# Graph attention over 200,000 edges: the one-hot matrix of the sums moves from matmul and ScalarE to compares on GpSimd, and queries shrink from 16 to 15 columns a head

## The chip, the cores and the metric

The kernel runs on one core of a Trainium2 chip. The metric is the device time of one execution in microseconds (us). A core has five engines that run beside each other and meet at semaphores: TensorE (PE in the profile, with PEld for its weight loads), VectorE (DVE), ScalarE (ACT), GpSimd (POOL) and SyncE (SP), which here only starts transfers. Sixteen DMA engines move data between HBM and SBUF.

## What is computed

A graph has 6250 nodes with 128 features and 200,000 edges with 128 features; `src` and `dst` name the ends of each edge, and the edges are sorted by `dst`. There are 8 heads of 16 columns.

```python
q = layer_norm(einsum('nf,hfd->hnd', x_node, Wq), gq, bq)      # k, v likewise; ke, ve from x_edge
rel_k = layer_norm(concatenate([ke, k[:, src]], -1) @ relk_W + relk_b, relk_g, relk_beta)
qk = sum(q[:, dst] * rel_k, -1) / 4.0
m = segment_max(qk.T, dst); se = segment_sum(exp(qk.T - m[dst]), dst)
lse = log(se) + m
rel_v = layer_norm(concatenate([ve, v[:, src]], -1) @ relv_W + relv_b, relv_g, relv_beta)
logw = qk - lse.T[:, dst]
agg = segment_sum(logw[..., None] * rel_v, dst)
z = layer_norm(relu(agg @ z_W + z_b), z_g, z_beta)
out = layernorm(x + z)
```

The inner layer norms remove the mean, so a head of 16 columns is held as 15 (`C = D - 1`, `HC = 8 * 15 = 120`). The 16th column of a query held the constant of the score, the part that comes from `relk_beta` and is the same for all edges of a node.

## The kernel before

Three phases follow each other: `start` (node projections, ranks, tables), `edges` (the loop over all edges) and `tail` (log-sum-exp, the folding of the sums, the output).

**The edge loop.** Edges are taken in 391 groups of 512 (`GROUPS`, four tiles of 128 edges). Each engine runs the same routine, `body(c)`, for one step after another, written out by hand in a fixed order; in step c it works on group c, c-1, ... as the pipeline asks. `PEEL` = 25 steps are written out, then a loop of 12 steps a turn, then the rest. Waits are semaphore counts; buffers are rings (`OR` = 6 one-hot matrices, `HR` = 6 results `hh`, `WR` = 4 weights `zw`).

For a group: PE transposes the edge features (L1159) and projects them twice (L1137). DVE scales the second projection to `p` (L1415), adds the gathered rows of the source nodes (L1395, group c-5), multiplies the key half by the expanded query (L1405, c-6), reduces sums of squares and products together (L1427, c-6), builds `hh`, which is what is summed over edges (L1432, c-9), and reduces the squares of the first projection (L1442, c-2). ACT squares, copies out of PSUM, and does the logarithms and exponentials.

**Queries by rank.** Within a tile the destination nodes are consecutive ranks. A DMA loads 128 rows of `q_by_rank` per tile (three bf16 parts each, `3 * F` = 384 columns), and 12 matmuls a group (L1195) expand them to edges with the one-hot matrix `oht` (ranks down, edges across), which one matmul (L1150) codes and ACT's Relu (L1225) makes.

**The sums.** The other orientation, `oh` (edges down, ranks across), serves as the weights of the matmuls that add `hh` up by rank (L1130, c-10). Before, four matmuls (L1188) code it in PSUM from three feature rows, and ACT's Relu (L1260) writes it to SBUF.

**GpSimd's step.** In `body(c)` GpSimd issues two indirect gathers (L1317, group c-3), multiplies the score into the weight, `w2` (L1330, c-9), forms the score without its constant, `qk0` (L1337, c-8), and issues the other two gathers of group c-3. DVE then adds the constant, which lies in column 15 of the product (L1389, c-9), and L1330 waits for that; DVE's L1432 waits for L1330:

```python
x = c - 9    # DVE, first in its step
v.tensor_tensor(out=hh[:, x % HR, :, :, 2 * C], in0=qk0[:], in1=z[:, x % ZR, :, 2 * H:3 * H, C], op=ALU.add)
...
dve.wait_ge(s_w2, n + 1)    # ahead of L1432
```

**In `start`**, nodes go in 25 pairs of 128-row blocks: ACT writes the first two bf16 parts of the query (L832, L839), and GpSimd scatters them to `q_by_rank` (L479). **In `tail`**, DVE forms `lse` in 13 turns (L1755).

Of the kernel before, what the change touches and what calls it, by code (L numbers as in the profile page):

```python
# [5 lines left out]
P = 128  # L6
# [42 lines left out]
def edge_attention(nc, a, out):  # L49
    f32, bf16, i32, u32 = mybir.dt.float32, mybir.dt.bfloat16, mybir.dt.int32, mybir.dt.uint32  # L50
    ctx = ExitStack()
    with ctx:
# [7 lines left out]
        q_rank = dram("q_by_rank", [QROWS, 3 * F], bf16)  # L60
# [35 lines left out]
        rank_i = sb_mid("first_rank", [1, ROWS], i32)  # L96
        nfeat = sb_mid("rank_code", [P, P], bf16)
# [5 lines left out]
                          first_pos=first_pos, sum_idx=sum_idx, degree=degree, carry_idx=carry_idx, w_edge=w_edge, cols=cols, rank_i=rank_i, nfeat=nfeat, feat=feat))  # L103
        def sb_late(name, shape, dt=f32):
# [7 lines left out]
                          w_edge=w_edge, cols=cols, rank_i=rank_i, nfeat=nfeat, feat=feat, eps_c=eps_c))  # L112
# [3 lines left out]
                         ones_row=ones_row, rows16=rows16, end_pos=end_pos, first_pos=first_pos, sum_idx=sum_idx, degree=degree), out)  # L116
# [21 lines left out]
def start(nc, a, t):  # L138
# [88 lines left out]
    room_b = sb("room_b", [P, BLOCKS * 3 * F // 2])  # L227
# [3 lines left out]
    qp = room_b[:].bitcast(bf16).rearrange("p (b f) -> p b f", f=3 * F)  # L231
# [23 lines left out]
    zero_q = sb("zero_q", [P, 3 * F], bf16)  # L255
# [9 lines left out]
    q1 = sb("n_q1", [P, 2, 2, F])  # L265
# [27 lines left out]
    s_u, s_tb, s_qs, s_q = sem("nodes_scaled"), sem("nodes_table"), sem("nodes_q_scaled"), sem("nodes_q")  # L293
    s_1, s_r1, s_2, s_3 = sem("nodes_part1"), sem("nodes_rest1"), sem("nodes_part2"), sem("nodes_part3")
# [23 lines left out]
    with nc.allow_non_contiguous_dma(reason="small weight and index layouts"), nc.Block(no_gpsimd_drain=True) as block:  # L318
# [82 lines left out]
        def _(pool):  # L401
# [69 lines left out]
            pool.reg_add(last_row, rows_less_2, 1)  # L471
            pool.wait_ge(s_idx, 1)
# [14 lines left out]
        def _(dve):  # L487
# [204 lines left out]
            for c in range(NP + 6):  # L692
                n = c - 4
                if pair(n):
                    b, nb, rows = pair(n)
                    dve.wait_ge(s_q, n + 1)
                    dve.wait_ge(s_1, n + 1)
                    if n >= 2:
                        dve.wait_ge(s_2, n - 1)
                        dve.wait_ge(s_3, n - 1)  # L700
                    v.tensor_tensor(out=q1[0:rows, n % 2, 0:nb, :], in0=q[0:rows, n % 3, 0:nb, :], in1=qp[0:rows, b:b + nb, 0:F], op=ALU.subtract).then_inc(s_r1, 1)
                n = c - 5
                if pair(n):
# [3 lines left out]
                    v.tensor_tensor(out=qp[0:rows, b:b + nb, 2 * F:3 * F], in0=q1[0:rows, n % 2, 0:nb, :], in1=qp[0:rows, b:b + nb, F:2 * F], op=ALU.subtract).then_inc(s_3, 1)  # L707
# [10 lines left out]
                if pair(n):  # L718
# [8 lines left out]
                    if n >= 3:  # L727
                        dve.wait_ge(s_1, n - 2)
                        dve.wait_ge(s_r1, n - 2)
# [26 lines left out]
        def _(act):  # L756
# [44 lines left out]
            for c in range(NP + 5):  # L801
# [20 lines left out]
                if pair(n):  # L822
# [4 lines left out]
                    sc_.activation(xt[:, n % 2, 0:nb, 0:rows], x_ps[:, 0:nb * F].rearrange("p (c n) -> p c n", c=nb)[:, :, 0:rows], ACT.Copy).then_inc(s_xc, 1)  # L827
                n = c - 4
                if pair(n):
                    b, nb, rows = pair(n)  # L830
                    act.wait_ge(s_r1, n + 1)
                    sc_.activation(qp[0:rows, b:b + nb, F:2 * F], q1[0:rows, n % 2, 0:nb, :], ACT.Copy).then_inc(s_2, 1)  # L832
                n = c - 3
                if pair(n):
# [4 lines left out]
                    sc_.activation(qp[0:rows, b:b + nb, 0:F], q[0:rows, n % 3, 0:nb, :], ACT.Copy).then_inc(s_1, 1)  # L839
# [5 lines left out]
        def _(pe):  # L845
# [68 lines left out]
            for c in range(NP + 1):  # L914
# [13 lines left out]
                if pair(n):  # L928
# [6 lines left out]
                    last.then_inc(s_xt, 1)  # L935
                if c == LB_AT:
                    pe.wait_ge(s_lb, 1)
# [10 lines left out]
def edges(nc, a, t):  # L948
# [16 lines left out]
    p = sb("e_p", [P, PR, TILES, H, 2, D])  # L965
    z = sb("e_z", [P, ZR, TILES, 3 * H, D])
# [4 lines left out]
    qk0 = sb("e_qk0", [P, TILES, H])  # L971
# [73 lines left out]
    with nc.Block(no_gpsimd_drain=True) as block:  # L1045
        @block.sync
        def _(sp):
# [8 lines left out]
            def body(c, i, loop):  # L1056
                if is_group(c, loop):
# [11 lines left out]
                    if c % BATCH == 0:  # L1069
                        b, kb = batch(c, i), (c // BATCH) % FB  # L1070
                        if loop or c >= BATCH * FB:
# [4 lines left out]
                            sp.wait_ge(s_ohp, used)  # L1076
# [38 lines left out]
        def _(pe):  # L1115
# [25 lines left out]
            def body(c, i, loop):  # L1141
                x = c - 4
                if is_group(x, loop):
                    n, kb = UNROLL * i + x, (x // BATCH) % FB
                    pe.wait_ge(s_ft[kb], 32 * (i + (x // BATCH) // FB + 1))
                    if loop or x >= 2:
                        pe.wait_ge(s_oh, n - 1)
                    elif x == 1:
                        pe.wait_ge(s_oht, 1)
# [31 lines left out]
                if is_group(x, loop):  # L1181
                    n, k, kb = UNROLL * i + x, x % QR, (x // BATCH) % FB
                    pe.wait_ge(s_oht, n + 2 if loop or x < GROUPS - 1 else n + 1)
                    if not loop and x == GROUPS - 1:
                        pe.wait_ge(s_oh, n)
# [949 lines left out]
```

## Time and profile before

| | us |
|---|---|
| median of 3 runs (lowest, highest) | 3037.59 (3036.09, 3039.39) |
| the profiled execution, its own time | 3036.29 |
| its span, first to last instruction | 3034.5 |
| DVE busy in the span | 2902.0 (96%) |
| PE busy in the span | 2843.7 (94%) |
| POOL busy in the span | 2407.3 (79%) |
| ACT busy in the span | 2306.7 (76%) |

Times of instructions come from the profiled execution. A row of the timeline gives start, duration, engine, line of the kernel, operation and operands, and in brackets the idle time ahead of it with what ended it. The recorded duration of an instruction reaches past the start of the next on the same engine (a DVE instruction of 960 elements is recorded at 1.15 to 1.34 us, and the next starts 1.07 us after it), so what an instruction costs its engine is the distance from start to start.

### The profile page before, as it was taken

What the parts mean: (1) busy time and instruction counts of PE and PEld (TensorE: products, weight loads), DVE (VectorE), ACT (ScalarE), POOL (GpSimd) and SP (SyncE); (2) the same over time, 40 slices, a digit from 0 to 9 for tenths busy, and PEclk for the clock granted to TensorE, in tenths of its full rate; (3) what the DMA queues carried; (4) which work ended last, traced back from release to release, by engine and by line L of the source; (5) the groups of instructions that cost most, each with busy time, mean ns of one, the idle gap of its engine ahead of it and who ended that gap; (6) DMA issues with size and microseconds to landing.
All of it is one profiled execution on the core that took longest, in us unless ns stands there. A gap on an engine that the chain in (4) does not pass through costs nothing. (4 is left out here: it accounts for less than half of the span.)

```text
span 3034.5 us, 76156 instructions
## 1 busy us (share of the span) xinstructions
PE 2843.7 (94%) x18870; PEld 2519.9 (83%) x18870; DVE 2902.0 (96%) x3459; ACT 2306.7 (76%) x5276; POOL 2407.3 (79%) x2622
## 2 busy tenths in 40 slices
PE   4669999999999999999999999999999999997945
PEld 3349999999999999999999999999999999995633
DVE  6879999999999999999999999999999999997957
ACT  2448888888888888888888888888888888885536
POOL 5768888888888888888888888888888888883773
PEclk9889999999999999999999999999999999998966
DMA  3568888888888888888888888888888888886642
GB/s 88 160 184 245 258 259 252 260 253 258 255 256 257 256 258 256 254 258 255 258 254 257 257 254 257 254 257 254 256 257 254 257 254 257 255 260 213 152 121 75
DMA packets 660921, 715.95 MB, mean 236 GB/s; under 512 B 97993, under 2 KB 554430, under 8 KB 660469
## 3 DMA queue, kind: packets, MB, share of 16 engines
q1 hardware_dynamic: 568201, 499.33, 52.3%
q0 software_dynamic: 84896, 211.42, 27.0%
q10 hardware_dynamic: 7756, 4.43, 0.6%
q8 instruction: 26, 0.43, 0.1%
q14 instruction: 42, 0.34, 0.0%
HBM read 482.62 MB, written 231.46 MB: 235 GB/s over the span
## 5 line engine op out<-in xcount | busy, mean ns | idle before, releaser
L1317 POOL DMA_INDIRECT e_rows<-node_table,e_gcol x1564 | 1933.0, 1236 | 422.6 <-issue 306.6
L1137 PE MATMUL banks<-w_edge,e_eat 128*128 128x240 f32 x6256 | 1396.5, 367 | 0.8 <-ACT e_ysq L1246 0.7
L1137 PEld LDWEIGHTS banks<-w_edge,e_eat 128*128 128x128 f32 x6256 | 1190.7, 191 | 87.6 <-issue 1.2
L1130 PE MATMUL banks<-e_h,e_oh 128*128 128x248 f32 x3128 | 805.5, 380 | 3.8 <-DVE e_h L1432 3.6
L1427 DVE TENSOR_REDUCE e_zs<-e_z 128x96 f32<-128x1440 f32 x391 | 671.6, 1718 | 0.2
L1130 PEld LDWEIGHTS banks<-e_h,e_oh 128*128 128x128 f32 x3128 | 534.6, 191 | 36.6 <-DVE e_h L1432 6.4
L1216 ACT ACTIVATE e_agg<-banks 128x496 f32<-128x496 f32 x782 | 453.8, 580 | 90.0 <-PE banks L1130 89.8
L1415 DVE TENSOR_TENSOR e_p<-banks,e_yr 128x960 f32<-128x960 f32 x391 | 479.4, 1226 | 5.0 <-PE banks L1137 4.3
L1395 DVE TENSOR_TENSOR e_p<-e_p,e_rows 128x960 f32<-128x960 f32 x391 | 479.6, 1227 | 0.0
L1432 DVE TENSOR_TENSOR e_h<-e_p,e_zw 128x960 f32<-128x960 f32 x391 | 478.5, 1224 | 1.2 <-POOL e_zw L1330 1.2
L1442 DVE TENSOR_REDUCE e_yvar<-e_ysq 128x64 f32<-128x960 f32 x391 | 477.2, 1221 | 0.0
L1225 ACT ACTIVATE e_oht<-banks 128x512 bf16<-128x512 f32 x391 | 233.4, 597 | 313.6 <-PE banks L1150 312.8
L1246 ACT ACTIVATE e_ysq<-banks 128x960 f32<-128x960 f32 x391 | 379.2, 970 | 51.5 <-PE banks L1137 6.4
L1239 ACT ACTIVATE e_z<-e_p 128x960 f32<-128x960 f32 x391 | 389.9, 997 | 6.1 <-DVE e_p L1395 5.0
L1195 PE MATMUL banks<-e_q,e_oht 128*128 128x128 bf16 x4692 | 326.5, 220 | 2.0 <-DVE e_z L1405 2.0
L1405 DVE TENSOR_TENSOR e_z<-e_p,banks 128x512 f32<-128x512 f32 x391 | 295.6, 756 | 0.1
L1195 PEld LDWEIGHTS banks<-e_q,e_oht 128*128 128x128 bf16 x4692 | 278.9, 98 | 2.5 <-issue 2.3
L1159 PEld LDWEIGHTS banks<-ident,e_ea 128*128 128x128 f32 x1564 | 195.5, 141 | 93.5 <-DMA e_ea<-in_edge_attr 24.2
L1159 PE MATMUL banks<-ident,e_ea 128*128 128x128 f32 x1564 | 235.8, 274 | 22.3 <-DMA e_ea<-in_edge_attr 22.3
L1231 ACT ACTIVATE e_eat<-banks 128x512 f32<-128x512 f32 x391 | 231.6, 592 | 17.5 <-PE banks L1159 17.4
L1260 ACT ACTIVATE e_oh<-banks 128x512 f32<-128x512 f32 x391 | 229.5, 587 | 0.0
L1188 PE MATMUL banks<-rank_code,e_feat 128*128 128x128 bf16 x1564 | 151.5, 220 | 0.0
(413 smaller groups left out, 2691.1 us busy)
## 6 DMA issues: line engine op xcount, KB each, us to landing
tile_sums<-e_agg SPq DMA_DIRECT2D x391, 496.0 KB
e_q<-q_by_rank SPq DMA_DIRECT2D x1564, 96.0 KB
e_ea<-in_edge_attr SPq DMA_DIRECT2D x390, 256.0 KB
e_rows<-node_table,e_gcol POOLq DMA_INDIRECT x1564
edge_lse<-t_lse_sb SPq DMA_DIRECT2D x14, 448.0 KB, 3.8
edge_qk<-e_qkt SPq DMA_DIRECT2D x130, 48.0 KB
node_table<-n_tb SPq DMA_DIRECT2D x24, 240.0 KB, 2.7
n_x<-in_x SPq DMA_DIRECT2D x24, 128.0 KB, 2.2
```

Of the source, the lines that this page charges most:

```text
L1130: last = nc.tensor.matmul(sums_bank(x, loop, half)[:, (j % 2) * AW:(j % 2 + 1) * AW], oh[:, x % OR, j, :], hh[:, x % HR, j, :, :].rearrang ...
L1137: last = nc.tensor.matmul(out_ps[:, j // 2, (j % 2) * 2 * HC:(j % 2 + 1) * 2 * HC], eat[:, x % 4, j * P:(j + 1) * P], t["w_edge"][:, at:at ...
L1159: last = nc.tensor.transpose(eat_ps[:, j * P:(j + 1) * P], ea[:, k, j, :], ident[:])
L1195: last = nc.tensor.matmul(qx_ps[:, j * F:(j + 1) * F], oht[:, x % 2, j * P:(j + 1) * P], qw[:, k, j, part * F:(part + 1) * F], start=(part ...
L1216: nc.scalar.activation(agg[:, k, 2 * half:2 * half + 2, :].rearrange("p j c -> p (j c)"), sums_bank(x, loop, half)[:, 0:2 * AW], ACT.Copy) ...
L1239: nc.scalar.activation(z[:, x % ZR, :, 0:2 * H, 0:C], p[:, k, :, :, :, 0:C].rearrange("p t h k c -> p t (h k) c"), ACT.Square).then_inc(s_ ...
L1317: g.indirect_dma_start(out=rows[:, k, j, :], out_offset=None, in_=table, in_offset=bass.IndirectOffsetOnAxis(ap=gcol[:, kb, at:at + 1].bit ...
L1395: v.tensor_tensor(out=p[:, k, :, :, :, 0:C].rearrange("p t h k c -> p (t h k) c"), in0=p[:, k, :, :, :, 0:C].rearrange("p t h k c -> p (t ...
L1415: v.tensor_tensor(out=p[:, k, :, :, :, 0:C].rearrange("p (b t) h k c -> p b (t h k) c", b=2), in0=u_ps.rearrange("p b (h c) -> p b h c", c=C),
L1427: v.tensor_reduce(out=zs[:, x % WR, :, :], in_=z[:, x % ZR, :, :, 0:C], axis=AX.X, op=ALU.add).then_inc(s_z, 1)
L1432: v.tensor_tensor(out=hh[:, x % HR, :, :, 0:2 * C].rearrange("p t h (s c) -> p (t h) s c", s=2), in0=p[:, k, :, :, 1, 0:C].rearrange("p t ...
L1442: v.tensor_reduce(out=yvar[:, x % 2, :, :], in_=ysq[:, x % 2, :, :].rearrange("p t (h c) -> p t h c", c=C), axis=AX.X, op=ALU.add).then_in ...
```

## The change

1. **One-hot by compare.** `start` keeps each edge's rank within its tile as bytes, edges down the partitions (`ranks`): 13 PE transposes in 4 sets, an ACT copy for each set, and two small fills by GpSimd. The edge loop loads 12 columns of them per batch of three groups (a third small DMA beside those for `feat` and `gcol`), ACT turns them to fp32 once a batch (`rcol`), and GpSimd makes `oh` with four `tensor_scalar` compares a group of a row 0..127 against each edge's rank. The four coding matmuls and ACT's Relu for it go.
2. **15 columns.** `q_by_rank` holds `3 * HC` = 360 columns, the expanded query 480 columns a group and not 512, and DVE's product L1405 works on 480.
3. **The constant by node.** DVE's add L1389 goes; GpSimd's product writes the score straight into `hh`. `start` keeps the constant of each node (`q_beta`, one small ACT copy per pair), and `tail` adds and subtracts it in `lse` (two more small DVE instructions a turn).

```diff
@@ start
+                if 0 <= k4 < RANK_SETS:
+                    act.wait_ge(s_rkt, k4 + 1)
+                    sc_.activation(t["ranks"][:].rearrange("e (p k) -> e k p", k=KT)[:, k0:k1, :],
+                                   bank[7][:, 0:(k1 - k0) * P].rearrange("e (k p) -> e k p", p=P), ACT.Copy).then_inc(s_rkc, 1)
...
+                    sc_.activation(t["q_beta"][0:rows, b:b + nb, :], q4[:, :, :, C], ACT.Copy).then_inc(s_qb, 1)
...
+                    for k in range(4 * k4, min(4 * k4 + 4, KT)):
+                        last = nc.tensor.transpose(bank[7][:, (k % 4) * P:(k % 4 + 1) * P], rank[:, k, :], ident[:])
@@ edges, SyncE
+                        sp.dma_start(rcol_i[:, kb, :], t["ranks"][:, bass.ds(BATCH * TILES * b, BATCH * TILES)]).then_inc(s_ft[kb], 16)
@@ edges, TensorE
-                    for j in range(TILES):
-                        at = (x % BATCH) * GE + j * P
-                        last = nc.tensor.matmul(misc[:, j * P:(j + 1) * P], feat[:, kb, at:at + P], t["nfeat"][:], start=True, stop=True)
-                    last.then_inc(s_ohp, 1)
...
-                            last = nc.tensor.matmul(qx_ps[:, j * F:(j + 1) * F], oht[:, x % 2, j * P:(j + 1) * P],
-                                                    qw[:, k, j, part * F:(part + 1) * F], start=(part == 0), stop=(part == 2))
+                            last = nc.tensor.matmul(qx_ps[:, j * HC:(j + 1) * HC], oht[:, x % 2, j * P:(j + 1) * P],
+                                                    qw[:, k, j, part * HC:(part + 1) * HC], start=(part == 0), stop=(part == 2))
@@ edges, ScalarE
-                    nc.scalar.activation(oh[:, x % OR, :, :].rearrange("p j n -> p (j n)"), misc, ACT.Relu).then_inc(s_oh, 1)
+                if is_group(x, loop) and x % BATCH == 0:
...
+                    nc.scalar.activation(rcol[:, kb, :], rcol_i[:, kb, :], ACT.Copy).then_inc(s_rf, 1)
@@ edges, GpSimd (after L1330)
+                x = c - 7
+                    pool.wait_ge(s_rf, batch(x, i) + 1)
+                    if loop or x >= OR:
+                        pool.wait_ge(s_agg, 2 * (n - OR) + 2)
                 x = c - 8
                     pool.wait_ge(s_zr, n + 1)
-                    g.tensor_tensor(out=qk0[:], in0=zs[:, x % WR, :, 2 * H:3 * H], in1=zr[:, x % WR, :, 0:H], op=ALU.mult).then_inc(s_qk0, 1)
+                    g.tensor_tensor(out=hh[:, x % HR, :, :, 2 * C], in0=zs[:, x % WR, :, 2 * H:3 * H], in1=zr[:, x % WR, :, 0:H], op=ALU.mult).then_inc(s_qk, 1)
+                x = c - 7
+                    for j in range(TILES):
+                        last = g.tensor_scalar(out=oh[:, x % OR, j, :], in0=iota_r[:], scalar1=rcol[:, kb, at + j:at + j + 1], scalar2=None, op0=ALU.is_equal)
+                    last.then_inc(s_oh, 1)
                 gathers(c - 3, i, loop, 2)
@@ edges, VectorE
-                    v.tensor_tensor(out=hh[:, x % HR, :, :, 2 * C], in0=qk0[:], in1=z[:, x % ZR, :, 2 * H:3 * H, C], op=ALU.add).then_inc(s_qk, 1)
...
-                                    in1=qx_ps.rearrange("p (t h d) -> p t h d", t=TILES, d=D), op=ALU.mult).then_inc(s_pq, 1)
+                                    in1=qx_ps[:, 0:TILES * HC].rearrange("p (t h c) -> p t h c", t=TILES, c=C), op=ALU.mult).then_inc(s_pq, 1)
@@ tail, VectorE
-                    v.tensor_tensor(out=lse[rr, 0:nb, :], in0=l0[rr, 0:nb, :], in1=lln[rr, 0:nb, :], op=ALU.add).then_inc(s["lse"], 1)
+                    v.tensor_tensor(out=lsr[rr, 0:nb, :], in0=l0[rr, 0:nb, :], in1=lln[rr, 0:nb, :], op=ALU.add).then_inc(s["lsr"], 1)
+                    dve.wait_ge(s["lsr"], n + 1)
+                    v.tensor_tensor(out=lsf[rr, 0:nb, :], in0=lsr[rr, 0:nb, :], in1=qb, op=ALU.add).then_inc(s["lsf"], 1)
+                    dve.wait_ge(s["lsf"], n + 1)
+                    v.tensor_tensor(out=lse[rr, 0:nb, :], in0=lsf[rr, 0:nb, :], in1=qb, op=ALU.subtract).then_inc(s["lse"], 1)
```

## Rows read from the trace of the kernel before

**Rows 1.** Busy time by stage, the steady part of the edge loop.

```profile
232.00:2746.00 2514.00, 2512.45 (x17387) 2287.16 (x17386) 2513.31 (x2689) 2072.20 (x4732) 2092.56 (x2305) 1.00 0.86 256
```

The columns are the window, its length, the busy us (and instructions) of PE, PEld, DVE, ACT and POOL, the granted TensorE clock, the busy share of the DMA engines, and GB/s.

**Rows 2.** Timeline of DVE over one step of the loop.

```profile
1498.87 1.34 DVE L1395 TENSOR_TENSOR e_p<-e_p,e_rows 128x960 f32<-128x960 f32 x1
1499.94 0.87 DVE L1405 TENSOR_TENSOR e_z<-e_p,banks 128x512 f32<-128x512 f32 x1
1500.53 1.34 DVE L1415 TENSOR_TENSOR e_p<-banks,e_yr 128x960 f32<-128x960 f32 x1
1501.60 1.83 DVE L1427 TENSOR_REDUCE e_zs<-e_z 128x96 f32<-128x1440 f32 x1
1503.16 1.34 DVE L1432 TENSOR_TENSOR e_h<-e_p,e_zw 128x960 f32<-128x960 f32 x1
1504.23 1.33 DVE L1442 TENSOR_REDUCE e_yvar<-e_ysq 128x64 f32<-128x960 f32 x1
1505.30 0.39 DVE L1389 TENSOR_TENSOR e_h<-e_qk,e_z 128x32 f32<-128x32 f32 x1
1505.42 1.34 DVE L1395 TENSOR_TENSOR e_p<-e_p,e_rows 128x960 f32<-128x960 f32 x1
```

**Rows 3.** Timeline of POOL over the same step.

```profile
1501.12 0.30 POOL L1330 TENSOR_TENSOR e_zw<-e_h,e_zw 128x32 f32<-128x32 f32 x1
1501.36 0.26 POOL L1337 TENSOR_TENSOR e_qk<-e_zs,e_zr 128x32 f32<-128x32 f32 x1
1501.78 1.04 POOL L1317 DMA_INDIRECT e_rows<-node_table,e_gcol  x1 [0.16 <-issue]
1503.12 1.02 POOL L1317 DMA_INDIRECT e_rows<-node_table,e_gcol  x1 [0.30 <-issue]
1504.45 1.01 POOL L1317 DMA_INDIRECT e_rows<-node_table,e_gcol  x1 [0.30 <-issue]
1505.77 1.87 POOL L1317 DMA_INDIRECT e_rows<-node_table,e_gcol  x1 [0.30 <-DVE e_h L1389]
1507.66 0.29 POOL L1330 TENSOR_TENSOR e_zw<-e_h,e_zw 128x32 f32<-128x32 f32 x1
```

**Rows 4.** Timeline of POOL and DVE, the filling of the loop.

```profile
219.03 1.01 POOL L1317 DMA_INDIRECT e_rows<-node_table,e_gcol  x1 [0.30 <-issue]
219.15 1.15 DVE L1395 TENSOR_TENSOR e_p<-e_p,e_rows 128x960 f32<-128x960 f32 x1
...
229.92 2.08 POOL L1317 DMA_INDIRECT e_rows<-node_table,e_gcol  x1 [0.30 <-issue]
...
229.96 1.15 DVE L1395 TENSOR_TENSOR e_p<-e_p,e_rows 128x960 f32<-128x960 f32 x1
```

**Rows 5.** Timeline of POOL and DVE, the draining of the loop.

```profile
2765.00 0.28 POOL L1330 TENSOR_TENSOR e_zw<-e_h,e_zw 128x32 f32<-128x32 f32 x1 [1.22 <-DVE e_h L1389]
2765.31 1.16 DVE L1432 TENSOR_TENSOR e_h<-e_p,e_zw 128x960 f32<-128x960 f32 x1 [0.40 <-POOL e_zw L1330]
2765.89 0.69 POOL L1337 TENSOR_TENSOR e_qk<-e_zs,e_zr 128x32 f32<-128x32 f32 x1 [0.61 <-ACT e_zr L1290]
```

**Rows 6.** Timeline of POOL in the first phase.

```profile
8.95 0.29 POOL L419 TENSOR_SCALAR_AFFINE_SELECT ident<-ident 128x128 f32<-128x128 f32 x1
9.20 0.19 POOL L421 TENSOR_SCALAR_AFFINE_SELECT sent<-sent 128x2 f32<-128x2 f32 x1
...
10.03 0.20 POOL L428 MEMSET tri<- 128x128 f32 x1
10.17 0.20 POOL L429 MEMSET ones<- 128x128 f32 x1
```

**Rows 7.** Groups of instructions by line: node stage, then the tail's line by itself.

```profile
L832 ACT ACTIVATE room_b<-n_q 128x256 bf16<-128x256 f32 x21 | 8.7, 417 | 1.0 <-DVE n_q L701 1.0
...
L1755 DVE TENSOR_TENSOR t_x<-t_x x13: 166/182/183, 2920.0 to 3007.8; 128x32 f32<-128x32 f32 x12, 106x8 f32<-106x8 f32 x1
```

In the second line the three numbers are the shortest, median and longest duration in ns.

More of the change, by code:

```diff
@@ L706, in _ @@
                     dve.wait_ge(s_2, n + 1)
-                    v.tensor_tensor(out=qp[0:rows, b:b + nb, 2 * F:3 * F], in0=q1[0:rows, n % 2, 0:nb, :], in1=qp[0:rows, b:b + nb, F:2 * F], op=ALU.subtract).then_inc(s_3, 1)
+                    v.tensor_tensor(out=qp[0:rows, b:b + nb, 2 * HC:3 * HC], in0=q1[0:rows, n % 2, 0:nb, :], in1=qp[0:rows, b:b + nb, HC:2 * HC], op=ALU.subtract).then_inc(s_3, 1)
                 n = c - 3
@@ L728, in _ @@
                         dve.wait_ge(s_1, n - 2)
+                        dve.wait_ge(s_qb, n - 2)
                         dve.wait_ge(s_r1, n - 2)
@@ L831, in _ @@
                     act.wait_ge(s_r1, n + 1)
-                    sc_.activation(qp[0:rows, b:b + nb, F:2 * F], q1[0:rows, n % 2, 0:nb, :], ACT.Copy).then_inc(s_2, 1)
+                    sc_.activation(qp[0:rows, b:b + nb, HC:2 * HC], q1[0:rows, n % 2, 0:nb, :], ACT.Copy).then_inc(s_2, 1)
                 n = c - 3
@@ L935, in _ @@
                     last.then_inc(s_xt, 1)
+                k4 = c - RANK_TURN
+                if 0 <= k4 < RANK_SETS:
+                    if k4 == 0:
+                        pe.wait_ge(s_wev, WEIGHTS)
+                        pe.wait_ge(s_rank, 1)
+                    else:
+                        pe.wait_ge(s_rkc, k4)
+                    for k in range(4 * k4, min(4 * k4 + 4, KT)):
+                        last = nc.tensor.transpose(bank[7][:, (k % 4) * P:(k % 4 + 1) * P], rank[:, k, :], ident[:])
+                    last.then_inc(s_rkt, 1)
                 if c == LB_AT:
+                    pe.wait_ge(s_rkc, RANK_SETS)
                     pe.wait_ge(s_lb, 1)
@@ L1182, in body @@
                     n, k, kb = UNROLL * i + x, x % QR, (x // BATCH) % FB
-                    pe.wait_ge(s_oht, n + 2 if loop or x < GROUPS - 1 else n + 1)
-                    if not loop and x == GROUPS - 1:
-                        pe.wait_ge(s_oh, n)
-                    for j in range(TILES):
-                        at = (x % BATCH) * GE + j * P
-                        last = nc.tensor.matmul(misc[:, j * P:(j + 1) * P], feat[:, kb, at:at + P], t["nfeat"][:], start=True, stop=True)
-                    last.then_inc(s_ohp, 1)
+                    pe.wait_ge(s_oht, n + 1)
                     pe.wait_ge(s_q[k], 64 * use(x, i, QR))
@@ L1238, in body @@
                         act.wait_ge(s_z, n - ZR + 1)
-                    nc.scalar.activation(z[:, x % ZR, :, 0:2 * H, 0:C], p[:, k, :, :, :, 0:C].rearrange("p t h k c -> p t (h k) c"), ACT.Square).then_inc(s_psq, 1)
+                    nc.scalar.activation(z[:, x % ZR, :, 0:2 * H, :], p[:, k, :, :, :, :].rearrange("p t h k c -> p t (h k) c"), ACT.Square).then_inc(s_psq, 1)
                 x = c - 1
@@ L1330, in body @@
                     g.tensor_tensor(out=zw[:, x % WR, :, :, 1], in0=hh[:, x % HR, :, :, 2 * C], in1=zw[:, x % WR, :, :, 0], op=ALU.mult).then_inc(s_w2, 1)
+                x = c - 7
+                if is_group(x, loop):
+                    n = UNROLL * i + x
+                    if not loop and x == 0:
+                        pool.wait_ge(s_iota, 1)
+                    pool.wait_ge(s_rf, batch(x, i) + 1)
+                    if loop or x >= OR:
+                        pool.wait_ge(s_agg, 2 * (n - OR) + 2)
                 x = c - 8
@@ L1352, in link @@
                 dve.wait_ge(s_ch, done[0])
-            dve.wait_ge(s_k, 5)
+            dve.wait_ge(s_k, 6)
+            v.tensor_copy(out=iota_r[:], in_=r_i).then_inc(s_iota, 1)
+            dve.wait_ge(s_iota, 1)
             link(v.tensor_tensor(out=ends[:, 1:2], in0=t["ends_f"][:, 1:2], in1=t["ends_f"][:, 0:1], op=ALU.not_equal))
@@ L1509, in tail @@
     la, ld = [small() for _ in range(2)], [small() for _ in range(2)]
-    lab, lex, lln, l0, lse = (small() for _ in range(5))
+    lab, lex, lln, l0, lsr, lsf, lse = (small() for _ in range(7))
     var, lnv = (small() for _ in range(2))
```

112 lines of the change are left out of this document (62 added, 50 removed).

## The prediction

> **What bounds the kernel now.** I read the busy time by stage first: the steady part of the edge loop is 2514 us of a span of 3034.5 us, and in it DVE is busy 2513.31 us [rows 1]. Its 2689 DVE instructions are 7 a step, so there are 384 steps of 2514 / 384 = 6.547 us. PE shows as much (2512.45 us), but its ends are modelled; ACT has 2072.20 us and POOL 2092.56 us, with clock 1.00 throughout. Then the timeline of DVE over one step [rows 2]: seven instructions without a gap, from start to start 1.07 (L1395), 0.59 (L1405), 1.07 (L1415), 1.56 (L1427), 1.07 (L1432), 1.07 (L1442) and 0.12 (L1389), together 6.55. DVE bounds the loop.
>
> The page makes POOL look 79% busy, with a fifth of its time to give. The timeline of POOL over the same step [rows 3] says otherwise. It has no wait for a partner's data: L1330 takes 0.24, L1337 with the gap behind it 0.42, then gathers at distances of 1.34, 1.33 and 1.32 (each 1.0 busy and 0.30 "issue", which the busy figure leaves out), and a fourth of 1.89. The only elastic part is that fourth, recorded at 1.87 where the others take 1.02. It starts at 1505.77, inside DVE's L1395, which runs from 1505.42 for 1.07. The timeline of the filling shows the same when POOL comes at other phases [rows 4]: a gather that starts 0.12 ahead of L1395 takes 1.01, one that starts 0.04 ahead takes 2.08. So a POOL instruction whose read of SBUF falls into a DVE instruction with two SBUF inputs stands still until that has finished. The draining shows it for an ordinary POOL instruction against L1432, the other DVE instruction of that kind [rows 5]: L1337 takes 0.69 and not 0.26, ending at 2766.58, 0.20 after L1432's 1.07 us are over. Without such a stop POOL's step is 0.24 + 0.42 + 1.34 + 1.33 + 1.32 + 1.05 = 5.70 us (1.05 is the free gather of 1.02 with the 0.02 or 0.03 that follows it): true slack 0.85 us a step, less what the stops take.
>
> The Trainium skill (SBUF — State Buffer, "Who interferes with whom") has this rule: a VectorE instruction with two SBUF inputs contends with a GpSimd instruction that reads SBUF, and whichever is second waits for the whole of the first. The rows agree for POOL as the second (0.69 for 0.26). The rule speaks against putting more reading instructions on POOL; without it the sum would be the third case below.
>
> **The change part by part.**
>
> *DVE.* L1389 goes, 0.12 a step. L1405 falls from 512 to 480 elements; between it and L1395, 448 elements make 1.07 − 0.59 = 0.48, so 32 make 0.03. DVE's step becomes 6.55 − 0.15 = 6.40: 384 × 0.147 = 56 us less, if DVE stays the bound.
>
> *PE and ACT.* PE loses four coding matmuls and 8 of 128 columns in twelve others, ACT an eviction of 512 columns a group against one tiny conversion per three groups. Neither sets the step; I give both nothing, and the saving only leaves them more room. PE's busy share falls if the step grows; at clock 1.00 it has room even then.
>
> *SP and DMA.* One more small load per three groups, rows of 720 bytes and not 768. The loads run ahead by several groups: nothing.
>
> *POOL.* Four compares of 128x128 are added. The trace has none. Nearest is the affine select of 128x128, one input and no second: 0.25 from its start to the next instruction [rows 6]. Below lies a fill of the same size, which reads nothing, 0.14; above, something beyond 0.25 for fetching a scalar per partition, for which the trace has no row; I take up to 0.40, half more than the select, as the upper bound. With 0.25: the free step becomes 5.70 − 0.42 + 0.24 + 4 × 0.25 + 0.16 = 6.68 (the 0.16 is the gap ahead of a gather). That is over DVE's 6.40 before any stop. POOL becomes the bound unless a compare costs under (6.40 − 5.68) / 4 = 0.18 all told.
>
> *Where the stalls go.* With POOL late, what is late next is DVE's L1432, which waits for L1330. Behind it on DVE stand L1442 and the next L1395. Take L1330's start as zero. L1432 starts at 0.31 [rows 5] and holds the read until 1.38. POOL's score product, at 0.24, is already under way. The first compare would start at 0.48, inside L1432: it stands until 1.38. Then four compares of 0.25 end at 2.38, and the gather is ready at 2.38 + 0.16 = 2.54. Meanwhile DVE has gone on: L1432, L1442, then L1395 from 0.31 + 2 × 1.07 = 2.45. The gather comes 0.09 too late and stands behind L1395: it ends 2.04 after L1395's start, as in the filling (2.08 from 0.04 ahead), at 4.49. Then 0.30 of issue, 1.33, 1.32 and the free 1.05 bring the next L1330 to 8.49. So the step is 8.49 us and repeats itself: DVE has only 6.40 us of work and waits 2.1 us each time at L1432, then starts the very instruction that stops the compares. The compare's cost drops out of this sum within bounds: the gather escapes only if it starts 0.12 ahead of L1395, so 1.38 + 4C + 0.16 below 2.33, C below 0.20; and if C is over (2.45 − 1.38) / 3 = 0.36, the last compare also falls behind L1395. The 0.04 or so that the first compare may need after the stop, and L1330's own variations, are within 0.2 us a step; the range of this case is 8.3 to 9.1 (at C = 0.40: 3.52 + 0.40 + 0.16 + 1.34 + 1.33 + 1.32 + 1.05 = 9.12).
>
> On the price of a compare the Trainium skill (GPSIMD Engine Reference, "Elementwise — side-by-side cycle accounting") gives 1.8 cycles at 1.2 GHz for each element in a tight loop, so as an estimate 128 × 1.8 / 1.2 = 192 ns and dispatch on top; no run here shows a compare. By that alone the sum would be the same, since C would stay between the two bounds.
>
> *Start and tail.* `start` gains 25 small ACT copies and four larger ones. If all were on the path at L832's 0.417, that is 12 us; DVE's part gets 16 columns narrower. `tail` gains 26 DVE instructions of 0.182 at most [rows 7], 4.7 us, in a stage where DVE often waits. I take 4 + 3 = 7 us, between 0 and 15.
>
> *The sum.* Against the profiled execution's own 3036.3 us (1.3 below the median, which is of no account here): 3036.3 + 384 × (8.49 − 6.547) + 7 = 3036.3 + 746 + 7 = 3789, and I say 3790.
>
> **The rivals.**
>
> *One stop, not two.* If compares cost under 0.20, or DVE resumes a little later so that the gather slips in ahead of L1395, only L1432's stop remains: with C = 0.20, 1.38 + 0.80 + 0.16 + 1.34 + 1.33 + 1.32 + 1.05 = 7.38; from 7.1 (C = 0.14) to 8.1 if steps of both kinds mix. Times 3256 to 3640, at 7.38 3363. For it: the margin is only 0.09 us. Against it: a compare has more to fetch than the select.
>
> *POOL bounds, without stops.* If compares, unlike the 32-element product, are not held up or only held for an instant, the step is 6.68 and the time 3036.3 + 384 × 0.133 + 7 = 3094. Against it: both kinds of POOL instruction in the rows were stopped.
>
> *The other side: faster.* The place is POOL's step: if a compare costs like a fill, 0.14, and the stops fall where a gather is already past its read, as the gather at 1503.12 is against L1432 at 1503.16 in rows 2 and 3, POOL needs 5.68 + 0.56 = 6.24, and DVE's 6.40 decides: 3036.3 − 56 + 7 = 2987. It decides below C = 0.18. Against it: L1330 and the compares are then four to six short reads in a row, and DVE's two instructions cover 2.14 of every 6.40 us.
>
> *No change.* The gain on DVE and a POOL step that happens to be 6.5 cancel: a narrow band.
>
> *Dearer compares.* C over 0.40 gives more than 4025 us.
>
> **How the numbers follow.** Chances: two stops 0.50; one stop 0.22; POOL without stops 0.10; faster 0.12; no change 0.02; dearer 0.04. The likeliest gives 3790, its own range is 3036.3 + 7 + 384 × (8.3 to 9.1 − 6.547), 3716 to 4024. Of the whole, a range from 3090, which takes in POOL's bound without stops, to 4030 leaves out the faster case, no change and the dearest, 0.18. A measurement of this kernel can tell about 0.2% from no change; faster by more than that 0.12, within it 0.02, slower 0.86.
>
> **What would show it.** If right, the profile after has DVE idle some 2 us a step ahead of L1432, released by POOL's L1330; POOL without a free moment beside its issue gaps; the first compare of four recorded at about 1.2 us and the others at about 0.3; one gather of four at about 2.0; PE and ACT idle a quarter. The compares' distances give C itself. If compares run at 0.14 to 0.18 and DVE stays gapless at 6.40, the prediction is wrong at the price of a compare; if they cost 0.25 but never show 1 us, it is wrong at the stop; if DVE waits for gathered rows and not for L1330, the phase that I worked out, and so the 8.49, is wrong.

## The result and the profile after

The kernel after takes 4258.19 us (4254.99 to 4260.55, 4 runs) where the kernel before takes 3037.78: 1.4018 of it, 95% interval 1.4000 to 1.4035. The direction was forecast, the size was not: 3790 us, with 4030 as the upper end. A step of the edge loop went from 6.547 us to 9.70 us; 384 × (9.70 − 6.547) = 1211 us, and that is all but 10 of the difference.

Four lines of the page of the kernel after; the groups are line, engine, operation and operands, then busy us and mean ns, then the idle time ahead with its releaser.

```profile
PE 3196.8 (75%) x17319; PEld 2655.6 (62%) x17319; DVE 3018.5 (71%) x3094; ACT 2170.2 (51%) x5045; POOL 3635.4 (85%) x4189
...
L1346 POOL DMA_INDIRECT e_rows<-node_table,e_gcol x1564 | 1624.9, 1039 | 425.2 <-issue 391.3
...
L1380 POOL TENSOR_SCALAR e_oh<-e_iota,e_rcol 128x128 f32<-128x128 f32 x1564 | 1549.3, 1001 | 0.0
...
L1467 DVE TENSOR_TENSOR e_h<-e_p,e_zw 128x960 f32<-128x960 f32 x391 | 594.3, 1520 | 1103.9 <-POOL e_zw L1359 1103.9
```

VectorE has fallen from 96% to 71%, and nearly all its idle time is one wait, 1103.9 us ahead of L1467 (L1432 before), for GpSimd's L1359 (L1330 before): 2.8 us a step. The compares are recorded at 1.0 us each. The gathers, which took 1236 ns on the mean, now take 1039: they are no longer the ones that are held.

The timeline of POOL over one step of the kernel after, to set beside [rows 3]:

```profile
2010.39 0.29 POOL L1359 TENSOR_TENSOR e_zw<-e_h,e_zw 128x32 f32<-128x32 f32 x1
2010.63 0.26 POOL L1375 TENSOR_TENSOR e_h<-e_zs,e_zr 128x32 f32<-128x32 f32 x1
2010.87 3.97 POOL L1380 TENSOR_SCALAR e_oh<-e_iota,e_rcol 128x128 f32<-128x128 f32 x4
2015.00 1.11 POOL L1346 DMA_INDIRECT e_rows<-node_table,e_gcol  x1 [0.17 <-issue]
2016.42 1.02 POOL L1346 DMA_INDIRECT e_rows<-node_table,e_gcol  x1 [0.30 <-issue]
2017.74 1.01 POOL L1346 DMA_INDIRECT e_rows<-node_table,e_gcol  x1 [0.31 <-issue]
2019.06 1.01 POOL L1346 DMA_INDIRECT e_rows<-node_table,e_gcol  x1 [0.30 <-issue]
2020.08 0.30 POOL L1359 TENSOR_TENSOR e_zw<-e_h,e_zw 128x32 f32<-128x32 f32 x1
```

POOL has no free moment beside its issue gaps; four compares fill 3.97 of 9.70 us. Whether that is their own cost or stops shows in shorter windows of POOL's timeline, which cut the merged row into single ones:

```profile
2010.87 0.61 POOL L1380 TENSOR_SCALAR e_oh<-e_iota,e_rcol 128x128 f32<-128x128 f32 x1
...
2010.87 1.85 POOL L1380 TENSOR_SCALAR e_oh<-e_iota,e_rcol 128x128 f32<-128x128 f32 x2
...
2011.46 1.84 POOL L1380 TENSOR_SCALAR e_oh<-e_iota,e_rcol 128x128 f32<-128x128 f32 x2
...
2013.28 1.55 POOL L1380 TENSOR_SCALAR e_oh<-e_iota,e_rcol 128x128 f32<-128x128 f32 x1
```

The group of these compares over the whole trace, by source line (shortest, median and longest ns):

```profile
L1380 POOL TENSOR_SCALAR e_oh<-e_iota,e_rcol x1564: 590/619/2248, 218.4 to 3981.5; 128x128 f32<-128x128 f32 x196
```

DVE's timeline of the same stretch, to set beside [rows 2]:

```profile
2010.72 1.52 DVE L1467 TENSOR_TENSOR e_h<-e_p,e_zw 128x960 f32<-128x960 f32 x1 [2.86 <-POOL e_zw L1359]
2012.17 1.14 DVE L1477 TENSOR_REDUCE e_yvar<-e_ysq 128x64 f32<-128x960 f32 x1
2013.23 1.14 DVE L1431 TENSOR_TENSOR e_p<-e_p,e_rows 128x960 f32<-128x960 f32 x1
2014.30 0.64 DVE L1440 TENSOR_TENSOR e_z<-e_p,banks 128x480 f32<-128x480 f32 x1
```

A compare that isn't held takes 0.59 from start to start (2010.87 to 2011.46). The second, from 2011.46, is held until L1467 ends at 2012.17, where the next VectorE instruction starts, and ends at 2012.72, 0.55 after it; the fourth starts at 2013.28, in L1431 (from 2013.23), and ends at 2014.83, 0.53 after it. VectorE loses as well: L1467 starts at 0.33 after L1359, but its successor comes 1.45 later and not 1.07, so it loses 0.38. So the walk for the kernel after, from L1359's start: product 0.24, first compare 0.48, L1467 really runs 0.71 to 1.78, second compare from 1.07, done at 2.31, third at 2.90, fourth held by L1431 (2.84 to 3.91), done at 4.44; then 0.17 and gathers at 4.61, 6.03, 7.35 and 8.67, and the next L1359 at 9.70. Compares of 0.59 and two stops of 0.64 and 0.96. The walk is fitted to this trace; the runs with two compares and with the compares last test it.

### The profile page after: what moved, and what is told of

Its sections match the earlier page's. It is cut to its first block and busy times, and to the rows that moved or that the text cites. A ratio compares the mean times of both kernels' runs of the same rounds, so it can differ in the third digit from the quotient of the medians.

```text
span 4255.3 us, 73823 instructions
## 1 busy us (share of the span) xinstructions
PE 3196.8 (75%) x17319; PEld 2655.6 (62%) x17319; DVE 3018.5 (71%) x3094; ACT 2170.2 (51%) x5045; POOL 3635.4 (85%) x4189
## 5 line engine op out<-in xcount | busy, mean ns | idle before, releaser
L1346 POOL DMA_INDIRECT e_rows<-node_table,e_gcol x1564 | 1624.9, 1039 | 425.2 <-issue 391.3
L1173 PE MATMUL banks<-w_edge,e_eat 128*128 128x240 f32 x6256 | 1597.8, 405 | 1.2 <-ACT e_ysq L1274 1.0
L1166 PE MATMUL banks<-e_h,e_oh 128*128 128x248 f32 x3128 | 943.1, 429 | 863.8 <-DVE e_h L1467 861.7
L1380 POOL TENSOR_SCALAR e_oh<-e_iota,e_rcol 128x128 f32<-128x128 f32 x1564 | 1549.3, 1001 | 0.0
L1173 PEld LDWEIGHTS banks<-w_edge,e_eat 128*128 128x128 f32 x6256 | 1341.6, 215 | 145.6 <-issue 1.6
L1467 DVE TENSOR_TENSOR e_h<-e_p,e_zw 128x960 f32<-128x960 f32 x391 | 594.3, 1520 | 1103.9 <-POOL e_zw L1359 1103.9
L1166 PEld LDWEIGHTS banks<-e_h,e_oh 128*128 128x128 f32 x3128 | 582.2, 207 | 998.4 <-issue 886.8
L1450 DVE TENSOR_TENSOR e_p<-banks,e_yr 128x960 f32<-128x960 f32 x391 | 447.5, 1144 | 4.1 <-PE banks L1173 4.1
L1431 DVE TENSOR_TENSOR e_p<-e_p,e_rows 128x960 f32<-128x960 f32 x391 | 446.8, 1143 | 1.0 <-DMA e_rows<-node_table,e_gcol 1.0
L1223 PE MATMUL banks<-e_q,e_oht 128*128 128x120 bf16 x4692 | 349.3, 231 | 4.7 <-DVE e_z L1440 4.2
L1440 DVE TENSOR_TENSOR e_z<-e_p,banks 128x480 f32<-128x480 f32 x391 | 250.6, 641 | 0.0
L1184 PE MATMUL banks<-e_feat,rank_code 128*128 128x512 bf16 x391 | 148.3, 379 | 0.0
```

The costliest lines, as they stand in the source:

```text
L1166: last = nc.tensor.matmul(sums_bank(x, loop, half)[:, (j % 2) * AW:(j % 2 + 1) * AW], oh[:, x % OR, j, :], hh[:, x % HR, j, :, :].rearrang ...
L1173: last = nc.tensor.matmul(out_ps[:, j // 2, (j % 2) * 2 * HC:(j % 2 + 1) * 2 * HC], eat[:, x % 4, j * P:(j + 1) * P], t["w_edge"][:, at:at ...
L1223: last = nc.tensor.matmul(qx_ps[:, j * HC:(j + 1) * HC], oht[:, x % 2, j * P:(j + 1) * P], qw[:, k, j, part * HC:(part + 1) * HC], start=( ...
L1346: g.indirect_dma_start(out=rows[:, k, j, :], out_offset=None, in_=table, in_offset=bass.IndirectOffsetOnAxis(ap=gcol[:, kb, at:at + 1].bit ...
L1380: last = g.tensor_scalar(out=oh[:, x % OR, j, :], in0=iota_r[:], scalar1=rcol[:, kb, at + j:at + j + 1], scalar2=None, op0=ALU.is_equal)
L1431: v.tensor_tensor(out=p[:, k, :, :, :, :].rearrange("p t h k c -> p (t h k c)"), in0=p[:, k, :, :, :, :].rearrange("p t h k c -> p (t h k ...
```

## The experiments

The experiments ran on four chips. On the first and the third the kernel before itself took longer (3223 us, 3182 to 3269 in 17 runs; 3154 us, 3145 to 3172 in 7) than on the second and the fourth (3036 and 3035 us). Steps that no transfer holds up can be compared across chips, the times of the first and third chip can't. A changed kernel whose time has no interval beside it ran once.

**A cheaper instruction in place of the compare: an affine select.**

```diff
-                        last = g.tensor_scalar(out=oh[:, x % OR, j, :], in0=iota_r[:], scalar1=rcol[:, kb, at + j:at + j + 1], scalar2=None, op0=ALU.is_equal)
+                        last = g.affine_select(out=oh[:, x % OR, j, :], in_=iota_r[:], compare_op=ALU.not_equal, fill=1.0, base=0, pattern=[[-1, P]], channel_multiplier=1)
```

> The kernel after, with each of the four compares replaced by an affine select of the same 128x128 (one input, 0.25 us in the trace of before; its result does not depend on the edge's rank, so the sums are not the reference's). Theory A, the prediction's walk with two stops: step 8.49 us, time about 3790 us. Theory A2, the same port rule with what the trace after shows in addition (VectorE's L1467 must itself wait until a compare's read is over, and is 0.4 us late): L1467 ends at 1.78 after L1359's start, only one select is held, the gather is ready at 2.64 and L1431 starts at 2.85, so one stop: step 7.68, time about 3480. Rival B (no port: POOL's own sum alone decides): step 6.68, time about 3100.

It took 3914.74 us on the first chip. The timeline of POOL over a step:

```profile
2009.16 0.30 POOL L1359 TENSOR_TENSOR e_zw<-e_h,e_zw 128x32 f32<-128x32 f32 x1
2009.40 0.27 POOL L1375 TENSOR_TENSOR e_h<-e_zs,e_zr 128x32 f32<-128x32 f32 x1
2009.61 1.99 POOL L1380 TENSOR_SCALAR_AFFINE_SELECT e_oh<-e_iota 128x128 f32<-128x128 f32 x4
2011.76 2.00 POOL L1346 DMA_INDIRECT e_rows<-node_table,e_gcol  x1 [0.16 <-issue]
2014.06 1.03 POOL L1346 DMA_INDIRECT e_rows<-node_table,e_gcol  x1 [0.30 <-issue]
2015.39 1.02 POOL L1346 DMA_INDIRECT e_rows<-node_table,e_gcol  x1 [0.31 <-issue]
2016.72 1.01 POOL L1346 DMA_INDIRECT e_rows<-node_table,e_gcol  x1 [0.30 <-issue]
2017.75 0.30 POOL L1359 TENSOR_TENSOR e_zw<-e_h,e_zw 128x32 f32<-128x32 f32 x1
```

The step is 8.59 us, where the prediction's walk has 8.49 and the walk with L1467 0.4 late has 7.68. Both stops are where they were predicted: four selects of 0.25 take 1.99 because L1467 holds the first, and the gather comes just too late and takes 2.00. My amendment of the walk was wrong for this instruction (L1467 is only 0.09 late here), and POOL's own sum, 6.68, is refuted.

**An instruction that reads nothing: a fill.**

```diff
+                        last = g.memset(oh[:, x % OR, j, :], 1.0)
```

> The kernel after, with each of the four compares replaced by a fill of the same size, which reads nothing (the one-hot matrix is all ones, so the sums are not the reference's). GpSimd's own step is 5.68 + 4 x 0.14 = 6.24 us, under VectorE's 6.40. Rival B (GpSimd's own sum and VectorE's alone): VectorE is the bound, step 6.40, time about 2990 us. Theory A (gathers stop behind VectorE instructions with two SBUF inputs): a slack of 0.16 us can't take a stop, so GpSimd still bounds, step 6.8 to 7.3, time 3140 to 3330.

It took 3383.25 us on the first chip, with a step of 7.21.

```profile
2013.16 0.30 POOL L1359 TENSOR_TENSOR e_zw<-e_h,e_zw 128x32 f32<-128x32 f32 x1
2013.40 0.27 POOL L1375 TENSOR_TENSOR e_h<-e_zs,e_zr 128x32 f32<-128x32 f32 x1
2013.59 0.64 POOL L1380 MEMSET e_oh<- 128x128 f32 x4
2014.39 1.22 POOL L1346 DMA_INDIRECT e_rows<-node_table,e_gcol  x1 [0.16 <-issue]
2015.91 1.80 POOL L1346 DMA_INDIRECT e_rows<-node_table,e_gcol  x1 [0.30 <-issue]
```

The fills themselves are not held, though L1467 runs over them; the gathers behind them are, 0.2 and 0.8 us. GpSimd's own sum was 0.16 below VectorE's, and it still became the bound: free slack under one stop is no slack.

**What in a compare costs 0.59?** Five kernels after with one thing changed each: the compare against a constant, a subtraction in its place, each compare as two of 64 columns, a plain copy, and the row 0..127 in bf16.

```diff
-... in0=iota_r[:], scalar1=rcol[:, kb, at + j:at + j + 1], scalar2=None, op0=ALU.is_equal)
+... in0=iota_r[:], scalar1=5.0, scalar2=None, op0=ALU.is_equal)
+... in0=iota_r[:], scalar1=rcol[:, kb, at + j:at + j + 1], scalar2=None, op0=ALU.subtract)
+... for half in (0, 64): out=oh[:, x % OR, j, half:half + 64], in0=iota_r[:, half:half + 64], ...
+last = g.tensor_copy(out=oh[:, x % OR, j, :], in_=iota_r[:])
+iota_r = sb("e_iota", [P, P], bf16)
```

> The kernel after, with the compare against the constant 5.0 and not against each edge's rank (so the one-hot matrix is not the reference's). Theory P (the 0.59 us of a compare come from fetching a scalar per partition): the compare falls to about 0.25 and the time to that of the select's run. Theory O (they come from the operation and its 128 elements): 0.55 to 0.6 as before, step 9.7, time about 4250 us.

> The kernel after, with the four compares as subtractions of the rank per partition (same operands, other operation; the one-hot matrix holds differences, so the sums are not the reference's). Theory O1 (the compare operation is what costs 0.59 against the affine select's 0.25): a subtraction costs 0.25 to 0.35, step about 8.5 to 8.7. Theory O2 (any tensor_scalar of this size costs it, whatever the operation): 0.59 and a step of 9.7.

> The kernel after, with each compare made as two of 64 columns (eight a group, same result). Cost fixed per instruction: eight cost twice as much as four, GpSimd's step grows by 2.4 us to about 12. Cost by element: an instruction of 64 costs a little over 0.3 us and the step stays within 0.5 of 9.7.

> The kernel after with each compare replaced by a plain copy of the same 128x128 (same input, no scalar; the one-hot matrix holds the numbers 0 to 127, so the sums are not the reference's). Theory S (the 0.53 to 0.59 us belong to tensor_scalar, not to reading and writing 128 elements): 0.25 a copy as for the affine select, and its step of 8.6. Rival R (any copy-like instruction of this size costs it): 0.5 and more, step 9.4 to 9.7.

> The kernel after with the row 0..127 that the compares read kept in bf16 (exact, same result). Rival: if the width of the input is part of a compare's 3 ns per element, a compare falls below 0.59 and the step below 9.5. Theory: it is the instruction's own loop, so 0.59 and 9.7 stay.

The group's own row in each of the five, in that order (shortest, median and longest ns):

```profile
L1380 POOL TENSOR_SCALAR e_oh<-e_iota x1564: 527/530/1548, 284.1 to 4163.1; 128x128 f32<-128x128 f32 x196
```

```profile
L1380 POOL TENSOR_SCALAR e_oh<-e_iota,e_rcol x1564: 592/621/2236, 221.2 to 3986.9; 128x128 f32<-128x128 f32 x196
```

```profile
L1381 POOL TENSOR_SCALAR e_oh<-e_iota,e_rcol x3128: 430/432/2378, 220.8 to 4440.1; 128x64 f32<-128x64 f32 x196
```

```profile
L1380 POOL COPY e_oh<-e_iota x1564: 279/283/1268, 219.8 to 3543.9; 128x128 f32<-128x128 f32 x196
```

```profile
L1380 POOL TENSOR_SCALAR e_oh<-e_iota,e_rcol x1564: 590/619/2247, 219.7 to 3982.2; 128x128 f32<-128x128 bf16 x196
```

| in place of the compare | time, us | step, us | median ns |
|---|---|---|---|
| (kernel after) | 4258.19 | 9.70 | 619 |
| constant, not a scalar per partition (first chip) | 4460.18 | 10.0 | 530 |
| subtraction | 4260.84 | 9.70 | 621 |
| two halves of 64 columns | 4713.23 | 10.86 | 432 |
| row 0..127 in bf16 | 4259.40 | 9.70 | 619 |
| plain copy | 3815.29 | 8.58 | 283 |

The cost is the instruction's, not the comparison's and not that of moving 128 elements: the affine select and the copy do the same elements for 0.23 to 0.25. The scalar per partition is no part of it either. With the constant the compare is recorded at 530 ns, but single rows of POOL's timeline show idle time between the compares, and from the second to the third start it is the same 0.59:

```profile
2011.51 1.34 POOL L1380 TENSOR_SCALAR e_oh<-e_iota 128x128 f32<-128x128 f32 x1
...
2012.91 0.53 POOL L1380 TENSOR_SCALAR e_oh<-e_iota 128x128 f32<-128x128 f32 x1
...
2013.50 1.46 POOL L1380 TENSOR_SCALAR e_oh<-e_iota 128x128 f32<-128x128 f32 x1
...
2015.02 0.53 POOL L1380 TENSOR_SCALAR e_oh<-e_iota 128x128 f32<-128x128 f32 x1
```

These rows also say why its step is 10.0 and not 9.70. The first compare starts 0.34 after L1375 where it is 0.24, the gap ahead of the gather is 0.28 where it is 0.17, and the two stops, now on the first and third compare, are 0.81 and 0.93 in place of 0.64 and 0.96.

A half that isn't held costs 0.41 from start to start:

```profile
2014.07 0.43 POOL L1381 TENSOR_SCALAR e_oh<-e_iota,e_rcol 128x64 f32<-128x64 f32 x1
...
2014.48 1.29 POOL L1381 TENSOR_SCALAR e_oh<-e_iota,e_rcol 128x64 f32<-128x64 f32 x1
```

So 64 elements cost 0.18 us, or 2.8 ns each, and 0.23 is fixed. The half-size run fell between its two expectations, since two fifths of a compare are fixed.

The runs differ in who gives way at L1467. Where the first instruction behind L1375 isn't held (the compare, the subtraction, the bf16 row), L1467 loses 0.38. Where that instruction is held (the constant, the halves, the copy, the select), L1467 loses 0.05 to 0.09. No run shows what decides it: the constant's compare starts 0.1 later than the kernel's own, but the first half starts at the same 0.47 after L1359 as the whole compare does, and is held.

The copy is also the prediction's sum at nearly its own price: 0.23 to 0.24 apiece, step 8.58, time 3815.29 us, where 8.49 and 3790 were forecast.

**Two compares in place of four.**

```diff
-                    for j in range(TILES):
+                    for j in range(2):
```

> The kernel after with two of the four compares a group (the other two quarters of the one-hot ring are filled with ones once, so the sums are not the reference's). Theory A, the walk with a compare at 0.59 and the port held by L1467 from 0.71 to 1.78 after L1359's start: second compare done at 2.31, gather ready at 2.47, ahead of L1431 at 2.84, so not held; the next gather at 3.81 held for 0.1 only; next L1359 at 7.56, time about 3430. Rival (four compares of 0.97 apiece, no stops: each compare costs its distance in the trace after): 9.70 - 2 x 0.97 = 7.76 with no gather of over 1.15 us; rival without any stop, at 0.59: 6.84, time about 3150.

The other two quarters of the ring are filled with ones once, ahead of the loop. The step is 7.58 us (L1360 at 2004.68 and 2012.26), as the walk has it, 7.56, where compares of 0.97 apiece without stops would have made it 7.76. No gather takes over 1.11 us. The time, 3525.46 us, is that of the third chip and can't be set against the 3430 expected.

**The four compares behind the second pair of gathers.**

```diff
+                gathers(c - 3, i, loop, 2)
                 x = c - 7
                 if is_group(x, loop):
...
-                gathers(c - 3, i, loop, 2)
```

> The kernel after with the four compares behind the second pair of gathers (same result). Theory A: the two stops stay but fall on gathers: ready at 0.66 and held by L1467 until 1.42, ready at 2.69 and held by L1431 until 3.56, then four compares of 0.59 unheld, step 9.45, about 4160 us; two gathers a step of 1.7 to 1.9 us and four compares together of 2.4. Rival (the compares themselves cost 0.97): still 4.0 us for the four, step 9.7 or over.

```profile
2008.02 0.29 POOL L1359 TENSOR_TENSOR e_zw<-e_h,e_zw 128x32 f32<-128x32 f32 x1
2008.26 0.26 POOL L1375 TENSOR_TENSOR e_h<-e_zs,e_zr 128x32 f32<-128x32 f32 x1
2008.67 1.79 POOL L1346 DMA_INDIRECT e_rows<-node_table,e_gcol  x1 [0.15 <-issue]
2010.76 1.79 POOL L1346 DMA_INDIRECT e_rows<-node_table,e_gcol  x1 [0.30 <-issue]
2012.60 2.35 POOL L1381 TENSOR_SCALAR e_oh<-e_iota,e_rcol 128x128 f32<-128x128 f32 x4
```

The step is 9.55 (9.45 expected), the time on the third chip 4283.19 us. The same two stops have moved to the gathers, and the four compares, unheld, take 2.35 us, 0.59 each. So 0.59 is theirs and the rest of the 3.97 was stops.

**The change without its first part.** The one-hot matrix comes again from four matmuls and a Relu; 15 columns and the constant by node are kept.

```diff
+                    for j in range(TILES):
+                        at = (x % BATCH) * GE + j * P
+                        last = nc.tensor.matmul(misc[:, j * P:(j + 1) * P], feat[:, kb, at:at + P], t["nfeat"][:], start=True, stop=True)
...
+                    nc.scalar.activation(oh[:, x % OR, :, :].rearrange("p j n -> p (j n)"), misc, ACT.Relu).then_inc(s_oh, 1)
...
-                        last = g.tensor_scalar(out=oh[:, x % OR, j, :], ...
```

> The change without its first part: the one-hot matrix again by four matmuls and ScalarE's Relu, no ranks in the first phase; queries of 15 columns and the constant by node kept. Theory: VectorE stays the bound and loses 0.15 us a step, GpSimd does as much as before: 3037 - 56 + 4 (start, tail) = 2985 us. Rival: GpSimd's score product, now ahead of L1432's data, or a stop at another phase costs more than the slack: 3037 or over.

> The kernel before, unchanged, for a profile beside the others of this call. Expected: VectorE without a gap, 6.55 us a step; if the loop shows waits for transfers here, they are the chip's and hold for its neighbours too.

> As in the first run without the compares (one-hot by matmul and Relu; 15 columns and the constant by node kept), with the kernel before profiled on the same chip. Theory: VectorE's step falls from 6.55 to 6.40 and the time by 1.5 to 2%. Rival: what VectorE gives back is taken up by waits for TensorE, for the eviction of the sums or for transfers, and the ratio stays within 0.5% of 1.

On the first chip the ratio was 1.0029 (0.9985 to 1.0073), inconclusive. On the second it was 3020.95 us against 3036.08: 0.9952 (0.9938 to 0.9965). The kernel before gave 3035.89 us there, so no transfer was in its way. Faster, but by 15 us and not by the 52 expected. The next four runs ask why.

**One coding matmul in place of four**, in the kernel without compares and in the kernel before:

```diff
-                    for j in range(TILES):
+                    for j in range(1):
                         at = (x % BATCH) * GE + j * P
```

> The kernel without the compares (15 columns and the constant by node kept), with one of its four coding matmuls a group (three quarters of the one-hot matrix then come from what stood in PSUM, so the sums are not the reference's): TensorE's step is 3 x 0.055 = 0.17 us shorter. Theory T (TensorE bounds it at 6.49, right behind VectorE's 6.40): the step falls to about 6.40 and the time to 2985 to 2990. Rival (VectorE's waits come from elsewhere, transfers or ScalarE): no change from 3021.

> The kernel before with one of its four coding matmuls a group (three quarters of the one-hot matrix then come from what stood in PSUM). Theory: VectorE bounds the kernel before at 6.55, so nothing changes: 3036 within 0.2%. Rival: TensorE bounds it as well, and it gets faster.

> As the earlier run with one coding matmul and no compares, which fell on a chip where the store of the sums held things up. Theory T: TensorE bounds the kernel without compares at 6.49 a step, so with 0.17 us less of it the step is 6.40 and the time 30 us under that of the next run. Rival: no difference between the two.

> The kernel without the compares once more, beside the run with one coding matmul: 0.995 of the kernel before where transfers are not in the way, as before.

On the third chip the first of these took 3216.21 us, 1.0193 (1.0141 to 1.0245) of the kernel before: a miss, with ScalarE's eviction of the sums (L1228) waiting 120.9 us in 1000 for a releaser that the profile calls remote; in the kernel the only such wait there is for the store of earlier sums. So it says nothing of TensorE. The kernel before with one coding matmul gave 3140.67 there in one run, 4 us under the lowest of the seven unchanged ones, which spread over 27: no gain that can be told. The median distance of its L1330 rows from 300 to 2700 us, 6.55, is that of the unchanged kernel's, 6.54. On the fourth chip the pair is clean: 2973.26 us, 0.9795 (0.9779 to 0.9812), against 3021.26 us, 0.9954 (0.9937 to 0.9970). The stretch from 300 to 2700 us in the windows view (PE, PEld, DVE, ACT, POOL busy; clock; DMA share; GB/s), without compares and then with one coding matmul:

```profile
300.00:2700.00 2400.00, 2400.00 (x16693) 2182.57 (x16692) 2380.41 (x2212) 1988.19 (x4543) 1997.55 (x2212) 1.00 0.87 254
```

```profile
300.00:2700.00 2400.00, 2392.29 (x15848) 2147.54 (x15847) 2399.82 (x2256) 2025.50 (x4627) 1984.64 (x2252) 1.00 0.88 258
```

In the first TensorE has no gap and VectorE has 20 us of them; in the second it is the other way round. TensorE's step without the compares is 6.51 us (2400 us for 2212 / 6 = 368.7 steps), just under VectorE's old 6.547, and that is where the gain ends. Between the two runs lie 48 us, where 30 were expected.

## Why the prediction was right and wrong

*VectorE the bound before, POOL's true step 5.70.* Right as far as the runs test it: without the compares the loop follows VectorE and TensorE, and POOL's step does not show.

*VectorE's saving, 0.15 a step.* Right: with TensorE out of the way the step is 6.38 (2400 / (2256 / 6)), where 6.40 was forecast. "Neither sets the step; I give both nothing" was wrong for TensorE in the part that I costed at nothing: in the kernel without compares its step is 6.51, 0.04 under VectorE's old one. It made no difference to the kernel after, where POOL decides, but it decides what parts 2 and 3 bring alone.

*The price of a compare: the step that failed.* "Nearest is the affine select of 128x128 ... 0.25", with "up to 0.40" as the upper bound. It is 0.59. The select was the right neighbour by shape, not by instruction: what set the price was tensor_scalar's own 2.8 ns an element. What the prediction allowed beyond 0.25 "for fetching a scalar per partition" measured nothing. Four at 0.34 more are 1.36 us, but part of that disappears in the stops: by the prediction's own rule for dear compares the price makes the step 3.52 + 0.59 + 0.16 + 5.04 = 9.31, 0.82 of the 1.21 us by which the step missed (9.70 less 8.49). The Trainium skill's figure of 1.8 cycles an element (GPSIMD Engine Reference, "Elementwise — side-by-side cycle accounting"), a best case, does not hold for this instruction: 2.8 ns are 3.3 cycles at its 1.2 GHz.

*POOL becomes the bound, VectorE waits at L1432 for L1330.* Right: 1103.9 us of waiting there.

*Two stops.* Right in mechanism and in place, shown with the price that was assumed: 8.59 with the select and 8.58 with the copy against 8.49. With compares of 0.59 they fall on the second and fourth compare, and not on the first and the last. *VectorE's own delay: a second term, put at nothing.* The 0.39 left from 9.31 to 9.70 is nearly all of it this: the prediction has L1432 hold the read from 0.31 to 1.38, but L1467, with its two SBUF inputs, itself loses 0.38 where the first compare runs unheld. That it waits for a read of that compare is argued from the times, not shown.

*Start and tail, 7 us.* Right in size. Between the profiles of before and after, the first L1432 (L1467) comes 2.1 us later (234.3 and 236.4), and what follows the start of the last one is 4.2 us longer (267.3 and 271.5).

*The range.* Its upper end rested on 0.40 for a compare. The case that came is the last rival, dearer compares, which had a chance of 0.04. For an instruction with no row, a bound of half more than the nearest was too narrow; the price turned out 2.4 times the nearest.

*The rivals.* One stop was seen when only two compares are made (7.58). POOL without stops, and faster, were refuted: even four fills, 0.16 under VectorE's step by the sum, gave 7.21.

## What to carry to other kernels

Take an engine's free time from start-to-start distances, not from its busy share: GpSimd, shown at 79% busy, had 0.85 us a step to give, and in the trace one stop filled it; the rest of its idle time was issue gaps. Before moving work to GpSimd, time that very instruction there, since on the same 128 columns a copy and an affine select cost 0.23 to 0.25 us and a tensor_scalar 0.59; and count, for each reading instruction, a VectorE instruction with two SBUF inputs that may stand in its way, up to 1.07 us here. When a bound is trimmed, look how far behind the next engine is: two of the three parts of this change were worth 1.8% on VectorE and gave 0.5%, because TensorE's step was only 0.04 us under the old one, and the first part, which would have freed TensorE, put GpSimd in front.

## What the runs showed that I had not expected

The stops go both ways, and where an instruction that reads meets L1467 one side gives way: VectorE's L1467 loses 0.38 us where the compare behind L1375 runs unheld, and 0.05 to 0.09 where the instruction there is held. A fill is never held, though L1467 runs over all four; a gather is, if it starts inside such a VectorE instruction, and not if it has already started. That it is the gather's read of its indices that stands still is a guess that fits these rows.

The granted clock of TensorE averages 0.90 in the loop of the kernel after, where it was 1.00. It changes between its two levels, shown as 0.50 and 1.00, within a step: after 3.04 us of idle time ahead of L1166 at 2002.68 it is 0.50 from 2003.0 to 2007.7 us, and 1.00 from 2009 to 2021. Eight projections take 3.40 us at the lower level and 1.78 at the upper. It cost next to nothing there: in the whole trace VectorE waited 4.1 us for projections (ahead of L1450), and ahead of L1467 for GpSimd alone.
